# The last tile of an eight-core linear-attention layer, its work put in another order

## The reference

```
h   = layernorm(x)
q,k,v = split(silu(causal_conv4(h @ W_qkv.T)))      # 16 heads of 64
q,k = l2norm(q)/8, l2norm(k);  z = h @ W_z.T
beta = sigmoid(h @ W_b.T);  g = -exp(A_log)*softplus(h @ W_a.T + dt_bias)
per token: S = S*exp(g) + k (v*beta)^T;  o = q S    # S is 64x64 per head
x = x + (o * rsqrt(mean(o*o)+1e-6) * silu(z)) @ W_out.T
h = layernorm(x);  x = x + h @ W_ffn (1024x1024, unfolded from small factors) + bias
```

## Time and profile before

| | us |
|---|---|
| median of 3 runs | 902.59 |
| lowest and highest | 896.23, 908.62 |
| the profiled execution | 901.92 |
| its span on core 0, the slowest | 899.8 |
| spans of the eight cores | 864.7 to 899.8 |
| TensorE busy, of the span | 656.8 (73%) |
| VectorE, ScalarE, GpSimd busy | 414.7, 338.2, 195.4 |

### The profile page before, as it was taken

One profiled execution on the slowest core, in us unless ns is written; L12 is line 12 of the kernel. 1 busy time (PEld: TensorE's weight loads), 2 busy tenths in 40 slices (PEclk: granted clock), 3 DMA queues, 4 the chain that ended last, 5 costly groups with the idle time before them and its releaser, 6 DMA issues.

```text
span 899.8 us, 14152 instructions; the slowest of 8 cores (864.7 to 899.8 us)
## 1 busy us (share of the span) xinstructions
PE 656.8 (73%) x4616; PEld 293.5 (33%) x4616; DVE 414.7 (46%) x681; ACT 338.2 (38%) x587; POOL 195.4 (22%) x231
## 2 busy tenths in 40 slices
PE   0675469999991089998853999869999997644563
PEld 0322134434440044443421444324444443322221
DVE  3533336666660146435410445783555662534432
ACT  0253335575661046454410465332544443111100
POOL 2020000000010000002121230541422551745310
PEclk9987889999996589999975999988999999666777
DMA  6699459989999999978789765866856757444321
GB/s 149 151 203 192 145 127 281 233 225 229 219 224 81 62 199 224 224 203 145 171 205 136 220 159 152 187 177 134 207 140 165 203 138 123 72 106 107 83 82 35
DMA packets 177247, 146.62 MB, mean 163 GB/s; under 512 B 119574, under 2 KB 140268, under 8 KB 177040
## 3 DMA queue, kind: packets, MB, share of 16 engines
q1 hardware_dynamic: 166416, 123.51, 59.1%
q0 software_dynamic: 10752, 22.13, 15.0%
HBM read 111.39 MB, written 18.56 MB: 144 GB/s over the span
## 4 chain that ended last, share of the span: by engine, by line
PE 43%; DMA 23%; DVE 9%; issue 9%; ACT 7%; SPq 7%; POOL 1%; DVEq 0%; ACTq 0%; POOLq 0%
PE pRG L501 22%; DMA dscr<-s_d 6%; PE pRG L548 6%; DMA s_lnxT<-s_lnx 5%; DMA wscr<-s_w 5%; SPq L131 4%; PE pRG L932 3%; PE pA L974 3%; SPq L136 3%; PE pB L932 3%; ACT s_post L554 2%; ACT L554 1%; DMA s_rb<-rscr 1%; DMA s_ktil<-s_post 1%; PE pRG L974 1%
## 5 line engine op out<-in xcount | busy, mean ns | idle before, releaser
L501 PE MATMUL pRG<-s_lnxT,s_w 128*128 128x512 bf16 x1408 | 340.0, 397 | 48.6 <-DMA s_w<-wcat 22.0
L501 PEld LDWEIGHTS pRG<-s_lnxT,s_w 128*128 128x128 bf16 x1408 | 136.8, 101 | 223.8 <-issue 80.6
L548 PE MATMUL pRG<-s_pre,s_d 128*128 128x512 bf16 x608 | 147.8, 382 | 8.6 <-ACT s_post L554 6.8
L554 ACT ACTIVATE s_post<-pRG 128x512 bf16<-128x512 f32 x152 | 86.0, 592 | 32.7 <-PE pRG L548 32.3
L857 POOL TENSOR_TENSOR s_S<-s_S,s_gam 128x512 f32<-128x512 f32 x32 | 33.4, 1045 | 262.5 <-DVE s_S L885 248.3
L525 ACT CAST s_pre<-pRG 128x512 bf16<-128x512 f32 x70 | 41.0, 586 | 121.5 <-PE pRG L501 120.7
L528 DVE CAST s_pre<-pRG 128x512 bf16<-128x512 f32 x82 | 56.3, 689 | 65.4 <-PE pRG L501 65.1
L412 ACT ACT_TABLE_LOAD x32 | 41.1, 1283 | 116.1 <-DVE s_pre L478 91.6
L548 PEld LDWEIGHTS pRG<-s_pre,s_d 128*128 128x128 bf16 x608 | 55.4, 98 | 81.4 <-issue 21.3
L746 DVE TENSOR_TENSOR s_ktil<-s_ktil,s_ekT 128x1024 bf16<-128x1024 bf16 x30 | 46.1, 1536 | 51.0 <-DMA s_ktil<-s_post 51.0
L554 ACT ACT_TABLE_LOAD x32 | 41.1, 1283 | 32.2 <-PE pRG L548 32.1
(11 more groups left out here) (157 smaller groups left out, 745.2 us busy)
## 6 DMA issues: line engine op xcount, KB each, us to landing
s_w<-wscr SPq DMA_DIRECT2D x144, 256.0 KB, 3.6
s_d<-dscr SPq DMA_DIRECT2D x128, 128.0 KB, 4.1
s_xa<-x SPq DMA_DIRECT2D x30, 512.0 KB, 5.2
s_w<-wcat POOLq DMA_DIRECT2D x32, 256.0 KB, 6.1
wscr<-s_w SPq DMA_DIRECT2D x32, 256.0 KB, 5.8
s_x<-x SPq DMA_DIRECT2D x14, 512.0 KB, 6.3
s_rb<-rscr POOLq DMA_DIRECT2D x24, 256.0 KB, 5.4
y<-s_x SPq DMA_DIRECT2D x12, 512.0 KB, 3.0
```

Of the source, the lines that this page charges most:

```text
L501: ins = P.e.matmul(ps, w[:, dc * 128:(dc + 1) * 128], lnxT[u % 2][:, dc, :], start=(dc == 0), stop=(dc == 7))
L548: ins = P.e.matmul(ps, dr[i % ND][:, tap * 128:(tap + 1) * 128], pre[:, j, tap:tap + 512], start=(tap == 0), stop=(tap == 3))
L554: silu_tok[(u, cc)] = ring_free[k] = S.mark(S.e.activation(out=post[u % 2][:, :, cc * 128:cc * 128 + 128], in_=ps.rearrange("p (a b) -> p ...
```

## The change

The order of the instructions in the last loop is another, and the last chunk has two functions of its own. `tvk(N0+1)` stands ahead of the loop and `tvk(n+2)` in round n. `ln2_rstd` and `ln2_norm` of chunk n-2 and `gate_out(n-1)` stand right behind `r_act(n)`; both halves of `decay(n+1)` follow, then `kscale(n+1)` and `qtil(n+1)`. `add_bias(n-2)` and `xr_load(n)` stand behind them. `outproj(n-1)` is followed by both halves of `qk(n+1)`, then `ln2_stats`, `ffn`, `y_store`. Behind the loop, `r_load(n)` and `gate_out(n)` of the last chunk stand ahead of the FFN of chunk n-1. `out_last` and `ffn_last` make the last chunk's products in halves of 512 columns, each half followed by its own addition; the last transposes are on TensorE and not by DMA; the last store is in two halves.

```diff
--- before.py
+++ after.py
@@ -286,7 +286,7 @@
         q_d, q_ds = slots("qd", ND), slots("qds", ND)
         q_xa, q_x2 = slots("qxa", 4), slots("qx2", 3)
         q_tr, q_tr2 = slots("qtr", 2), slots("qtq", 2)
-        q_y = slots("qy", 3)
+        q_y, q_yl = slots("qy", 3), slots("qyl", 2)
         q_c = slots("qc", 21)
         q_a, q_e = slots("qa", 1)[0], slots("qe", 4)
         q_b3 = slots("qb", 3)
@@ -983,6 +983,53 @@
         def y_store(n):
             Y.need(y_tok[n])
             yst_tok[n] = q_y[n % 3].go(Y, y[n * 128:(n + 1) * 128, :], x2[n % 3])
+
+
+        def out_last(n):
+            ps, fr = pair["C"]
+            P.need(*fr[0])
+            P.need(gat_tok[n])
+            bn = bnB[n % 2]
+            for hf in range(2):
+                hc = slice(hf * 512, hf * 512 + 512)
+                for cc in range(8):
+                    ins = P.e.matmul(ps[:, hc], buf("ga", n)[:, cc * 128:(cc + 1) * 128],
+                                     wout[:, cc, hc], start=(cc == 0), stop=(cc == 7))
+                V.need(P.mark(ins), x2ld_tok[n], norm2_tok.get(n - 2))
+                t = V.mark(V.e.tensor_tensor(out=x2[n % 3][:, hc], in0=ps[:, hc],
+                                             in1=x2[n % 3][:, hc], op=ALU.add))
+                V.need(t)
+                t = V.mark(V.e.bn_stats(out=bn[:, 6 * hf:6 * hf + 6], in_=x2[n % 3][:, hc]))
+            V.need(t)
+            t = rstd(bn, V.mark(V.e.bn_aggr(out=bn[:, 12:14], in_=bn[:, 0:12])))
+            V.need(t, l2_tok.get(n - 1))
+            t = norm2_tok[n] = V.mark(V.e.tensor_scalar(
+                out=ln2, in0=x2[n % 3], scalar1=bn[:, 12:13], scalar2=bn[:, 15:16],
+                op0=ALU.subtract, op1=ALU.mult))
+            P.need(t, *psB_free[0])
+            pb = pB[:, 0:512].bitcast(BF16)
+            for dc in range(8):
+                ins = P.e.transpose(out=pb[:, dc * 128:(dc + 1) * 128],
+                                    in_=ln2[:, dc * 128:(dc + 1) * 128], identity=i128b)
+            V.need(P.mark(ins), ffn_tok.get(n - 2))
+            l2_tok[n] = V.mark(V.e.tensor_copy(
+                out=ln2T[n % 2], in_=pb.rearrange("p (a b) -> p a b", a=8)))
+
+        def ffn_last(n):
+            ps, fr = pair["A"]
+            P.need(*fr[0])
+            P.need(l2_tok[n])
+            add_bias(n)
+            for hf in range(2):
+                hc = slice(hf * 512, hf * 512 + 512)
+                for dg in range(8):
+                    ins = P.e.matmul(ps[:, hc], ln2T[n % 2][:, dg, :], wbig[:, dg, hc],
+                                     start=(dg == 0), stop=(dg == 7))
+                V.need(P.mark(ins), xb_tok[n])
+                t = V.mark(V.e.tensor_tensor(out=x2[n % 3][:, hc], in0=ps[:, hc],
+                                             in1=x2[n % 3][:, hc], op=ALU.add))
+                Y.need(t)
+                q_yl[hf].go(Y, y[n * 128:(n + 1) * 128, hc], x2[n % 3][:, hc])
 
 
         def unfold():
@@ -1209,65 +1256,61 @@
         pair["D"][1][0] = [*(f if isinstance(f, list) else [f]), gate_free[0]]
         r_act(N0 - 1)
         ln2_rstd(N0 - 2)
+        kscale(4 * NPRE + N0)
+        ln2_norm(N0 - 2)
+        r_load(N0 - 1)
+        decay(N0, 0)
+        qtil(N0)
+        decay(N0, 1)
+        i51_load(N0 + 1)
+        add_bias(N0 - 2)
+        qk(N0, 0)
+        qk(N0, 1)
+        tvk(4 * NPRE + N0 + 1)
         for n in range(N0, N0 + 4):
             g = n + 4 * NPRE
             more = n < N0 + 3
-            if n == N0:
-                kscale(g)
-                r_load(n - 1)
-                ln2_norm(n - 2)
-                decay(n, 0)
-                qtil(n)
-                decay(n, 1)
-                i51_load(n + 1)
-                add_bias(n - 2)
-                qk(n, 0)
-                qk(n, 1)
-            else:
+            if n > N0:
                 r_load(n - 1)
             state_decay(g)
-            if more:
-                tvk(g + 1)
-            xr_load(n)
             oT(n, "C")
-            if more:
-                kscale(g + 1)
             state(g, "D")
             r_act(n)
+            if n > N0:
+                ln2_rstd(n - 2)
+                ln2_norm(n - 2)
+            gate_out(n - 1)
             if more:
                 decay(n + 1, 0)
-            gate_out(n - 1)
+                decay(n + 1, 1)
+                kscale(g + 1)
+                qtil(n + 1)
+                if n < N0 + 2:
+                    i51_load(n + 2)
+                    tvk(g + 2)
+            if n > N0:
+                add_bias(n - 2)
+            xr_load(n)
             outproj(n - 1, "C")
             if more:
-                qtil(n + 1)
-                decay(n + 1, 1)
-                if n < N0 + 2:
-                    i51_load(n + 2)
+                qk(n + 1, 0)
+                qk(n + 1, 1)
             ln2_stats(n - 1)
-            if more:
-                qk(n + 1, 0)
             ffn(n - 2, "D")
             y_store(n - 2)
-            if more:
-                qk(n + 1, 1)
-            ln2_rstd(n - 1)
-            ln2_norm(n - 1)
-            add_bias(n - 1)
         n = N0 + 3
         r_load(n)
+        ln2_rstd(n - 1)
+        ln2_norm(n - 1)
+        add_bias(n - 1)
+        gate_out(n)
         ffn(n - 1, "D")
         y_store(n - 1)
-        gate_out(n)
-        outproj(n, "C")
-        ln2_stats(n)
-        ln2_rstd(n)
-        ln2_norm(n)
-        add_bias(n)
-        ffn(n, "A")
-        y_store(n)
-
-
-        for q in (q_w + q_wc + q_ws + q_d + q_ds + q_xa + q_x2 + q_tr + q_tr2 + q_y + q_c + q_b3 + q_eb
+        out_last(n)
+        ffn_last(n)
+
+
+        for q in (q_w + q_wc + q_ws + q_d + q_ds + q_xa + q_x2 + q_tr + q_tr2 + q_y + q_yl + q_c + q_b3 + q_eb
                   + q_rb + q_e + q_tv + q_tk + q_r + [q_a, q_i]):
             if q.v > 0:
                 Y.need(q.tok)
```

## The result

The changed kernel takes 870.55 us (median of four runs, 867.81 to 880.4) against 903.17 for the kernel before, run beside it: a ratio of 0.9634, 95% interval 0.9564 to 0.9704. The forecast was 871. A second set of runs gave 871.56 us (867.3 to 875.59) and a ratio of 0.9604 (0.9536 to 0.9672).

What follows compares the result with a forecast made beforehand. Waits, not a full engine, bound the last tile, through k's transposes. Loop order gives -23.8 and the end 7.6, in all -31.4 from 901.9: 870.5 us, forecast 871; own range 862 to 876, 8 in 10 range 859 to 886.

Steps and rivals of the forecast that it cites:

- The basis: Last tile: no engine is full, waits bound it; middle rounds' chain runs through k's transposes, 7.30 us from issue to landing.
- Rival (c): Last tile: each wait is met by another of its size, only the end's 7.6 and round 16's 1.7 gained: 893; chance 0.09.
- Round 16: First round of the last loop: copy ends at 768.7 instead of 770.4, projection at 777.8, chunk 17's copy at 786.3.
- both terms that I had kept at their high row: Round 16: the index rows' load kept at 6.5 us and the projection at 5.62.
- 12.2 + w: One later round, copy of the norms' sums to the next: chain of 12.2 us plus projection w, together 17.1.
- w: Projection time in a later round: 4.94 us taken, 3.61 and 6.42 kept for the range.
- The end: From chunk 19's copy at 820.5 to the last addition at 860.5; 7.6 of the 31.4 us gained here.
- The recorded range of 862 to 876: Whole kernel: the forecast's own range in us, given as w from 3.61 to 6.42.
- rival (a): TensorE's clock stays up: projections and FFN 18 at 3.61, last FFN 1.5 shorter; 39.7 saved, 862; chance 0.16.
- What costs nothing: Last loop: moved transposes, SP issues, add_bias and state scaling are covered; GpSimd's possible 3 us a round has some 5 to spare.
- (b): Last loop: GpSimd or loads replace k's transposes as the wait; rounds of 20 to 23, 880 to 889; chance 0.16.
- (d): SP's three transposes in a row and x's load block each other, 50 us lost: 921; chance 0.03.

Runs made afterwards that it cites:

- early-transposes kernel: Kernel before with only v's and k's transposes issued two chunks ahead: 908.72 us, ratio 1.0006, tail 144.4 against 144.2.
- the kernel with the filled gap: Changed kernel plus six products with overwritten result in TensorE's wait ahead of each projection of the last loop: 886.31 us, tail 112.7 against 113.0.
- with the gating first: Changed kernel with gate_out(n-1) ahead of rstd and norm of chunk n-2: 866.9 us, ratio 0.9533, tail 107.7 against 113.0.
- the two half kernels: New loop with old end: ratio 0.9563, tail 121.3; old loop with new end: 893.23 us, ratio 0.9856, tail 136.4; kernel before: tail 144.2.
- the version with the late statistics: Changed kernel with gate_out(n-1) ahead of rstd and norm, and ln2_stats(n-2) behind that gating: 867.54 us, ratio 0.9586, tail 110.5.

## Why the prediction was right, by its steps

**The basis.** Waits bounded the tail, not an engine: shown, since moving two loads alone took 14.6 us away at unchanged work. But I named only k's transposes as the wait of the middle rounds, and the early-transposes kernel is the test of that: nothing. The chain of waits shows the load that came last; the read-back of r, issued at nearly the same time, was right behind it. Rival (c) had named it as the wait that would come next, and in that half step it did. My sum was safe from this because it was laid on the new order, where both are covered.

**Round 16.** The copy came 1.8 us sooner on core 0 (1.7 forecast), 1.0 to 2.7 over the cores. The next round was to take 17.6 and took 15.5 or 15.6 on six cores: both terms that I had kept at their high row were lower. On core 2 the index rows landed 4.8 us after issue instead of 6.5, so the projection started 1.5 us behind the copy, not 3.5, and it took 4.83 for 5.62; what follows it took 9.1 for 8.5. That the input load goes out later and lets them through fits; it wasn't tried by itself.

**The later rounds.** 12.2 + w was forecast. On core 2 the rounds less their projections are 18.23 - 6.25 and 17.65 - 5.67, both 11.98. The term that was mis-sized is w: 4.94 was taken, 6.25, 5.67 and 5.38 came. The granted clock within these three is 0.57, 0.63 and 0.66, that is most of their time at the lower of the two levels; duration times clock is 3.56, 3.57 and 3.55, and the kernel with the filled gap has 3.61 at 1.00. So the clock alone accounts for w. I had priced w by the idle time ahead of it and the work around it, and the rows don't bear out a price by the gap: after 2.68 us idle the last projection of the kernel before took 3.61 on six cores and 5.30 on two, core 0 among them; with the gating first it took 5.78 after 0.52 on core 0. What decides stays open; for w there is a spread (5.0 to 6.5 over the cores in the three later projections of the change) and no rule here.

**The end.** 40.0 was forecast, 37.5 to 40.3 came. FFN 18 took 4.92 on core 2 where I had taken 6.42 (6.4 to 6.5 on cores 3, 5 and 7); the halves' additions took 0.69 as costed, the transposes 0.61 for 1.01. On core 2 the later rounds came 1.7 longer in all than forecast, the first round 2.1 and the end 2.4 shorter, so the tail was some 3 us shorter than its sum. That the time of the run met the forecast within 0.5 us is partly chance: the starts move it by more. The recorded range of 862 to 876 isn't that of w alone: three projections at 3.61 give 866.5; 862 needs both FFNs at the higher clock too, and is rival (a).

**What costs nothing.** Right for `add_bias`, the state's scaling and the SP queue. I had GpSimd waiting for VectorE, up to 3 us a round. That came, but smaller: in the next round its two selects took 3.46 where they took 2.14 in the first, the square 2.32 for 1.89, and GpSimd's busy time in the two later rounds is 12.7 and 12.2 us against 11.9 and 11.2 before (core 0). What I had not counted is VectorE's side: k's factor took 1.63 to 2.11 for 1.23, q's scaling 1.57 to 4.85 for 0.68, beside GpSimd's selects and square. Both were hidden behind the projection, so the sum held. The rule of the Trainium skill's page "SBUF — State Buffer", "SBUF: two separate sides", that the one who comes second blocks for the whole instruction, covers both directions. The trace agrees that VectorE can be the one who is blocked, but its 4.85 beside selects and square of 2.14 and 1.89 spans several of GpSimd's instructions and not one.

**Rivals.** (a), the clock stays up, needed 3.61 in each round and didn't come; core by core the end swings between 37.5 and 40.3, and the last FFN between 4.93 and 6.43 (cores 2 and 1). (b) didn't come in the change; in the version with the late statistics loads do take over, with waits of 0.75 to 2.06 us each on core 2, but its rounds stay under the 20 of that rival. (c) is refuted for the change by the two half kernels, (d) by rounds of 15 to 18 us.

## What to carry to other kernels

Where two loads are issued together, the chain of waits names one; before taking it away, look when the other lands and who stands behind it. A wait can be covered from in front: put behind it, on the same engine, nothing that the long products need. Judge an edit of one stage by that stage cut out of every core's trace when the rest of the kernel varies more than the edit is worth.

## What the runs showed that I had not expected

- VectorE's work can take as long as a run of GpSimd's instructions beside it: 0.68 became 4.85 and a norm of 0.81 became 4.75 us beside two selects and a square. Started ahead of the selects the same norm took 0.81.
- Shortening a wait ahead of TensorE can pay again in the clock, but not everywhere: halves in the end were worth 1.65 us of work and 1.3 us of faster products on core 0, while on the odd cores the last FFN was faster without them (4.90 to 4.96 against 5.30 to 6.43).
- The same code reached its tail 32 us apart on different cores of one execution (726.2 to 757.9 before), and at other cores in the next.
